# One merged scan per pair of states, a fourth ring group, and another order of feed-forward units around the output projection

## The reference

```python
# part 1: selective state space model, inner width 1024, 16 states
xz = x @ W_in + b_in;  u, z = split(xz);  u = silu(u)
B, C = split(u @ W_xproj + b_xproj);  dt = softplus(u @ W_dt + b_dt)
h[t] = h[t-1] * exp(dt[t] * A) + dt[t] * u[t] * B[t]      # per channel and state
y[t] = sum over states of h[t] * C[t] + D * u[t]
x = layernorm(x + (y * silu(z)) @ W_out + b_out)
# part 2: masked cross attention, 16 heads, context of 77
# part 3: x @ W1 + b1, plus gain * sin(theta + 0.1 * hidden), relu, @ W2 + b2
```

## Time and profile before

| | us |
|---|---|
| median of 3 timed runs (3167.78 to 3171.23) | 3168.35 |
| the profiled execution, device time | 3163.83 |
| its span, first to last instruction | 3162.1 |
| scan phase, first scan to last (from the trace) | 59.0 to 1964.2 |

### The profile page before, as it was taken

The page is one execution under the profiler, slowest core; times in us unless marked ns, Lnnn a source line. Parts: engine busy times, 40 slices in busy tenths (PEclk is TensorE's granted clock), DMA queues, the critical chain, the costliest instruction groups (busy, mean ns, idle before and its releaser), DMA issues. The chain is left out here.

```text
span 3162.1 us, 48953 instructions
## 1 busy us (share of the span) xinstructions
PE 2830.4 (90%) x18968; PEld 1268.4 (40%) x18968; DVE 2692.5 (85%) x3070; ACT 2015.1 (64%) x3616; POOL 1828.9 (58%) x944
## 2 busy tenths in 40 slices
PE   7878878978878888888889889989999999999998
PEld 2222222222222222222222223556666676667765
DVE  5899999999999999999999978766666677777776
ACT  6766776776776776776776745555555556655564
POOL 4788988978978988978988987311111111112100
PEclk9999999999999999999999989999999999999999
DMA  4111112112112111111112143701111000000000
GB/s 159 51 51 41 58 51 66 45 37 71 41 43 65 41 51 57 50 41 57 51 53 65 51 131 125 225 28 42 42 42 42 28 29 22 23 30 29 30 8 14
DMA packets 119976, 172.51 MB, mean 55 GB/s; under 512 B 13250, under 2 KB 48706, under 8 KB 119236
## 3 DMA queue, kind: packets, MB, share of 16 engines
q1 hardware_dynamic: 119748, 169.37, 16.5%
HBM read 100.66 MB, written 66.58 MB: 53 GB/s over the span
## 5 line engine op out<-in xcount | busy, mean ns | idle before, releaser
L852 POOL TENSOR_TENSOR h<-h,c_rep 128x1024 f32<-128x1024 f32 x511 | 1196.7, 2355 | 281.6 <-ACT carry L605 280.1
L756 DVE TENSOR_TENSOR_SCAN h<-r_ps,carry,h 128x512 f32<-128x512 f32 x768 | 938.9, 1262 | 10.6 <-ACT r_ps L599 10.4
L599 ACT ACTIVATE r_ps<-r_ps,decay 128x512 f32<-128x512 f32 x1024 | 631.7, 656 | 390.3 <-PE r_ps L361 389.8
L743 DVE TENSOR_TENSOR h<-u_ps,b_rep 128x1024 f32<-128x1024 f32 x512 | 614.0, 1199 | 48.0 <-PE u_ps L374 47.4
L374 PE MATMUL u_ps<-dtu,spread 32*128 32x512 f16 x2048 | 319.5, 390 | 105.3 <-DVE h L743 105.0
L361 PE MATMUL r_ps<-dt,spread 32*128 32x512 f16 x2048 | 316.9, 387 | 49.7 <-DVE h L756 43.1
L390 PE MATMUL y_ps<-h,gather 128*32 128x512 f32 x2048 | 288.4, 637 | 65.8 <-POOL h L852 64.7
L1882 POOL TENSOR_TENSOR o_in<-o_in,rows 128x1024 f32<-128x1024 f32 x15 | 37.0, 2464 | 508.9 <-DMA o_in<-o_dram 508.9
L756 DVE TENSOR_TENSOR_SCAN h<-r_ps,zero,h 128x512 f32<-128x512 f32 x256 | 313.1, 1263 | 7.1 <-ACT r_ps L599 7.0
L40 PE MATMUL fps<-x,region 128*128 128x256 f16 x1024 | 283.6, 277 | 3.4 <-issue 2.4
L41 PE MATMUL fps<-x,region 128*128 128x256 f16 x1024 | 283.0, 276 | 0.0
(11 more groups left out here) (260 smaller groups left out, 5635.0 us busy)
## 6 DMA issues: line engine op xcount, KB each, us to landing
u_t_dram<-u SPq DMA_DIRECT2D x16, 1024.0 KB, 4.7
uz<-u_t_dram SPq DMA_DIRECT2D x64, 256.0 KB, 4.0
z_t_dram<-zs SPq DMA_DIRECT2D x32, 512.0 KB, 3.0
uz<-z_t_dram SPq DMA_DIRECT2D x64, 256.0 KB, 4.1
y_t_dram<-y SPq DMA_DIRECT2D x64, 256.0 KB, 2.3
region<-y_t_dram SPq DMA_DIRECT2D x32, 256.0 KB, 3.3
result<-x SPq DMA_DIRECT2D x16, 512.0 KB, 2.8
x_t<-dram_x_t SPq DMA_DIRECT2D x15, 512.0 KB, 4.0
```

Source lines behind the costliest of these rows:

```text
L599: nc.scalar.activation(bank, bank, ACT.Exp, scale=decay[:, col:col + 1]).then_inc(s_da, 1)
L743: nc.vector.tensor_tensor(h[:, g % H_GROUPS, o:o + 2, :], u_ps[:, :, :], b_rep[:, c % 2:c % 2 + 1, :].broadcast_to([P, 2, TS]), ALU.mult). ...
L756: nc.vector.tensor_tensor_scan(row, r_ps[:, 2 * (pair % 2) + o, :], row, start, ALU.mult, ALU.add)\
L852: nc.gpsimd.tensor_tensor(rows, rows, c_rep[:, c % 2:c % 2 + 1, :].broadcast_to([P, 2, TS]), ALU.mult)\
```

## The change

In the scan phase, `scans` becomes one instruction of 1024 columns over both banks. Between the two rows the state must be cut and restarted. So PE writes zero into column 0 of the second bank's decays by a one-column matmul (`joint_decay_zero`), after the exponentials. In chunks that carry a state over, ACT first adds decay times carry into column 0 of the second row (`joint_column`). PE does this step after `produce` and before `sums` and `rep_dt`. The ring gets a fourth group, `sums` and `gate` come two pairs later, `y` is written over the z tile in `uz`, and `rep_dt` and `save_carry` count scans by the pair. In the second phase, bodies with `ops` move feed-forward steps of units 0 to 4 around the projection and the scores on PE, ACT and DVE, and `body(1)`'s loads and bias for chunk 2 are issued in `first()`.

```diff
-H_GROUPS = 3
+H_GROUPS = 4
+SUMS_BEHIND = 5
@@ SP: load_z
-                    sp.wait_ge(s_y, n - 1)
+                    sp.wait_ge(s_yout[n % 2], 16 * (n // 2))
@@ PE
                 if pair >= 2:
-                    pe.wait_ge(s_scan, 2 * pair - 2)
+                    pe.wait_ge(s_scan, pair - 1)
...
+            def joint_decay_zero(pair):
+                c, j, p = place(pair)
+                pe.wait_ge(s_da, 2 * pair + 2)
+                if c % PER_SEQ:
+                    pe.wait_ge(s_joint, joints(pair) + 1)
+                nc.tensor.matmul(r_ps[:, 2 * (pair % 2) + 1, 0:1], spread[0:32, 0, :], no_decay, start=True, stop=True)\
+                    .then_inc(s_cut, 1)
...
                     out_piece((s - OUT_AT) // 2, (s - OUT_AT) % 2)
-                if pair % 2 and pair >= 3:
-                    sums((pair - 3) // 2)
+                if pair + 1 < TOTAL:
+                    joint_decay_zero(pair + 1)
+                if pair % 2 and pair >= SUMS_BEHIND:
+                    sums((pair - SUMS_BEHIND) // 2)
                 if pair + 2 < TOTAL:
                     rep_dt(pair + 2)
+            sums(TOTAL // 2 - 2)
             sums(TOTAL // 2 - 1)
@@ ACT
+            def joint_column(pair):
+                c, j, p = place(pair)
+                if c % PER_SEQ == 0:
+                    return
+                act.wait_ge(s_da, 2 * pair + 2)
+                act.wait_ge(s_m1, pair + 1)
+                act.wait_ge(s_carry, pair - PAIRS + 1)
+                col = j * NSTATE + 2 * p + 1
+                at = h[:, pair // 2 % H_GROUPS, 2 * (pair % 2) + 1, 0:1]
+                nc.scalar.activation(at, r_ps[:, 2 * (pair % 2) + 1, 0:1], ACT.Identity, bias=at,
+                                     scale=carry[:, col:col + 1]).then_inc(s_joint, 1)
...
                     exps(pair + 2)
+                    joint_column(pair + 2)
@@ DVE
-                for o in range(2):
-                    col = j * NSTATE + 2 * p + o
-                    dve.wait_ge(s_da, 2 * pair + o + 1)
-                    row = h[:, pair // 2 % H_GROUPS, 2 * (pair % 2) + o, :]
-                    start = carry[:, col:col + 1] if c % PER_SEQ else zero[:, 0:1]
-                    nc.vector.tensor_tensor_scan(row, r_ps[:, 2 * (pair % 2) + o, :], row, start, ALU.mult, ALU.add)\
-                        .then_inc(s_scan, 1)
+                dve.wait_ge(s_cut, pair + 1)
+                o = 2 * (pair % 2)
+                col = j * NSTATE + 2 * p
+                rows = h[:, pair // 2 % H_GROUPS, o:o + 2, :].rearrange("p o t -> p (o t)")
+                start = carry[:, col:col + 1] if c % PER_SEQ else zero[:, 0:1]
+                nc.vector.tensor_tensor_scan(rows, r_ps[:, o:o + 2, :].rearrange("p o t -> p (o t)"), rows, start,
+                                             ALU.mult, ALU.add).then_inc(s_scan, 1)
...
-                if pair % 8 == 2 and pair >= 10:
+                if pair % 8 == 4 and pair >= 12:
                     gate(pair // 8 - 1)
@@ second phase, SP: first()
+                sp.wait_ge(s_x1, 1)
+                load(o_in[:, :, :], chunk_rows("o", 2), s_oin)
...
+                sp.wait_ge(s_rwo, NT)
+                load(x1[:, 0, :, :], chunk_rows("x", 2), s_xin)
@@ PE: body with ops
                         out_projection(c, m * NT + 1, sps)
+                    hidden(b, 2)
                     scores(c, 0, batch, (0, 1), ops)
+                    hidden(b, 3)
+                    scores(c, 0, batch, (2, 3), ops)
+                    second(b, 0)
+                    scores(c, 1, batch, (0, 1), ops)
+                    hidden(b, 4)
+                    scores(c, 1, batch, (2, 3), ops)
+                    second(b, 1)
@@ ACT: body, not late
-                    y_high(Y_PAIRED - 1)
                     weights_high(8)
                     weights_high(9)
+                    y_high(Y_PAIRED - 1)
@@ ACT: body with ops
+                    if not late:
+                        deviation("x1", 0, c + 2)
+                    sine(b, 0)
                     out_evacuated(m * NT, sps)
+                    sine(b, 1)
+                    relu(b, 0)
+                    relu(b, 1)
                     out_evacuated(m * NT + 1, sps)
+                    hid_out(b, 2)
+                    sine(b, 2)
+                    hid_out(b, 3)
+                    sine(b, 3)
+                    relu(b, 2)
+                    relu(b, 3)
+                    exps(c, 0)
+                    exps(c, 1)
+                    hid_out(b, 4)
@@ DVE: body with ops
+                    fraction(b, 0)
+                    fraction(b, 1)
+                    if not late:
+                        statistics("x1", 0, c + 1, x1[:, 1 - par, :, :])
+                        normalize("x1", 0, c + 1, x1[:, 1 - par, :, :])
+                    mix(b, 0)
+                    mix(b, 1)
+                    act_low(b, 0)
+                    act_low(b, 1)
                     masked(c, 0, (0, 1))
+                    fraction(b, 2)
                     masked(c, 0, (2, 3))
+                    row_maximum(c, 0)
+                    mix(b, 2)
+                    fraction(b, 3)
                     masked(c, 1, (0, 1))
+                    less_maximum(c, 0)
@@ POOL: first() and body
-                for i in range(1, Y_PAIRED - 1):
+                for i in range(1, Y_PAIRED - 2):
                     y_low(i)
+                o_bias(2)
+                y_low(Y_PAIRED - 2)
...
-                if more:
+                if more and late:
                     pool.wait_ge(s_avl, c * NT)
                     o_bias(c + 1)
...
+                if not late:
+                    for m in ops:
+                        y_low(m * NT + 1)
                 x2_bias(c - 1, 1 - par)
-                for m in ops:
-                    y_low(m * NT + 1)
```

More of the change, by code:

```diff
@@ L1356, in body @@
                     hidden(b, 1)
-                if front:
-                    scores(c, 0, batch, (2, 3), ops)
-                hidden(b, 2)
-                if front:
-                    scores(c, 1, batch, (0, 1), ops)
-                hidden(b, 3)
-                if front:
-                    scores(c, 1, batch, (2, 3), ops)
-                second(b, 0)
-                hidden(b, 4)
-                second(b, 1)
+                    if front:
+                        scores(c, 0, batch, (2, 3), ())
+                    hidden(b, 2)
+                    if front:
+                        scores(c, 1, batch, (0, 1), ())
+                    hidden(b, 3)
+                    if front:
+                        scores(c, 1, batch, (2, 3), ())
+                    second(b, 0)
+                    hidden(b, 4)
+                    second(b, 1)
                 hidden(b, 5)
@@ L1813, in body @@
                     normalize("w2", 2, d, x2[:, par, :, :])
[L1814 to L1816 removed]
+                    if more:
+                        normalize("x1", 0, c + 1, x1[:, 1 - par, :, :])
+                if ops:
+                    fraction(b, 0)
+                    fraction(b, 1)
+                    if not late:
+                        statistics("x1", 0, c + 1, x1[:, 1 - par, :, :])
+                        normalize("x1", 0, c + 1, x1[:, 1 - par, :, :])
+                    mix(b, 0)
+                    mix(b, 1)
+                    act_low(b, 0)
+                    act_low(b, 1)
@@ L1839, in body @@
                     less_maximum(c, 1)
-                mix(b, 3)
-                fraction(b, 4)
-                act_low(b, 3)
+                    fraction(b, 4)
+                else:
+                    if front:
+                        masked(c, 0, (0, 1))
+                    fraction(b, 0)
+                    if front:
+                        masked(c, 0, (2, 3))
+                    fraction(b, 1)
+                    mix(b, 0)
+                    if front:
+                        masked(c, 1, (0, 1))
+                        row_maximum(c, 0)
+                    fraction(b, 2)
+                    act_low(b, 0)
+                    mix(b, 1)
+                    if front:
+                        masked(c, 1, (2, 3))
+                        less_maximum(c, 0)
+                    act_low(b, 1)
+                    fraction(b, 3)
+                    mix(b, 2)
+                    if front:
+                        row_maximum(c, 1)
+                    act_low(b, 2)
+                    if front:
+                        less_maximum(c, 1)
+                    mix(b, 3)
+                    fraction(b, 4)
+                    act_low(b, 3)
@@ L1922, in body @@
                     x1_sum(c + 1, 1 - par)
+                if not late:
+                    for m in ops:
+                        y_low(m * NT + 1)
                 x2_bias(c - 1, 1 - par)
-                for m in ops:
-                    y_low(m * NT + 1)
+                if late:
+                    for m in ops:
+                        y_low(m * NT + 1)
             all_chunks(pool, first, body)
```

67 lines of the change are left out of this document (27 added, 40 removed).

## The result

| | before | after |
|---|---|---|
| median of 4 timed runs, us | 3168.07 (3164.61 to 3171.23) | 3217.91 (3213.28 to 3221.38) |
| profiled execution, us | 3163.83 | 3213.28 |
| scan phase, first scan to last | 1905.2 | 1981.9 |

The ratio is 1.0157, 95% interval 1.0139 to 1.0174: the change makes the kernel 1.6% slower. 3132 was forecast, with a range up to 3185. The phases moved in opposite directions: the scan phase took 76.7 us more, the second phase (from the last scan to the end) 25.6 us less.

What follows compares the result with a forecast made beforehand. DVE was taken to set the scan phase's pace and PE to bound its last pairs and the second phase. -56 - 30 + 67 + 5 - 14 - 8 = -36 us gave 3132 us, range 3070 to 3185.

Steps and rivals of the forecast that it cites:

- The merged scan: DVE, scan phase: one instruction start saved per pair, 0.116 us x 482 pairs = -56 us, bounds -17 and -90.
- Chain length: Scan phase, from the second exponential's end to the scan: 0.6 us, or 0.35 in chunks 0 and 4 without joint column.
- Most pairs have the decays one to three us early, so it is covered there: Scan phase: the new chain of 0.6 us is covered in most pairs, but not behind a SiLU.
- only a late ACT makes it wait: PE at the cut: it arrives 1.8 to 2.4 us after `rep_dt`, while exponentials and column need 1.5.
- The price of a SiLU: Scan phase: the new chain costs 1.2 us behind each of 56 SiLUs, +67 us, bounds +17 and +140.
- The walk through one burst: Scan phase from pair 35, worked through behind a SiLU: pair 38 is 1.1 us late, pair 39 0.6, the next burst 1.5.
- The fourth group, the later sums: Scan phase: sums two pairs later end PE's waits for POOL and DVE's for `u_ps`, -30 us, bounds -20 and -45.
- 30 of the 47.4: Scan phase: of DVE's 47.4 us of waits for `u_ps` from PE, 30 us were taken as saved.
- Moving `gate` and writing y over z cost nothing: Scan phase: `load_z` now waits for the store of y, but has over 27 us until its gate; no cost.
- PE at the end of the phase: Last 30 pairs of the scan phase, bound by PE: the cut costs 30 x 0.17 = +5 us.
- The second phase: Bodies with `ops`: holes before the scores and slow clock go, -14 us in bodies 2 to 6, -8 in body 1, together -22.
- The rival: Scan phase: the cut makes PE and ACT one queue at the slower side's pace; 2.5 us a SiLU, 3205 us, 13%.

Runs made afterwards that it cites:

- cut_two_scans: `sp_order` with the merged scan split into two of 512 columns that follow without a wait, cut and joint column kept: 3215.26 us, 1.0153.
- no_silu: `sp_order` with a plain copy in place of each SiLU and no table loads around it: 3100.96 us, 0.9791.
- two_scans_sp: After with two scans again, no cut or joint column, and in the last chunk the store of y behind the output tiles: 3124.58 us, 0.9877.
- sp_order: After with only SP's store of y in the last chunk moved behind the output tiles' traffic: 3202.58 us, 1.0117.
- act_zero: `sp_order` with the zero written by ACT behind its joint column instead of by PE's cut: 3194.73 us, 1.0091.
- ffn_only: The scan phase of before with the second phase of after: 3141.11 us, 0.9929.
- col_no_wait: `two_scans_sp`, first scan waiting for both exponentials, plus an ACT instruction of the joint column's shape on unused data that no scan waits for: 3159.42 us, 0.9978.

## Why the prediction was wrong

The failed steps are in the scan phase. The prediction held the new chain covered in most pairs and cheap behind a SiLU (1.2 us), and so counted the merged scan's saving in full. The runs showed a chain that is short of cover in far more pairs, about 2 us a SiLU, 11 of the forecast 56 us from merging, and 24 us in the last chunk from a queue that it hadn't looked at.

- **The merged scan** was sized well: its record is 2.342 us (2.33 forecast), an undisturbed pair 3.375 (3.36), so 0.106 us a pair are saved. Forecast were -56 us. The step that failed is "0.116 x 482 pairs": it assumed that DVE sets the pace afterwards too. `cut_two_scans` shows that 11 us arrive. The 157 ns that the prediction took from the Trainium skill ("VectorE: DVE Perf Modes", section on the TRN2 errata) did not show either: 106 ns are the measured return.
- **Chain length.** The sum said 0.6 us, the trace has 0.82, the median of the 106 pairs in which each step followed the one before at once. The 201 ns of `save_carry` were the wrong row for the joint column: it takes 351. The hand-over behind it took 0.145 and the one from the cut to the scan 0.137, not 0.05. The exponential that they were read from ends at 679.80 in the trace, 0.13 before its scan and not under 0.1. Without the joint column the forecast 0.35 stands beside 0.34. For the cut itself 0.17 was right (0.163 to 0.166).
- **"Most pairs have the decays one to three us early, so it is covered there"** and "only a late ACT makes it wait" put the chain at nothing outside the bursts. In chunks 2 to 6 of after PE stood behind the joint column 153 times, in the 256 pairs that have one. Without any SiLU 7.9 us of excess a chunk are left (`no_silu`), where `two_scans_sp`, without the chain but with its SiLUs, has 2.9.
- **The price of a SiLU**, 1.2 us x 56 = +67, is the term that was mis-sized. Two numbers bear on it: 2.0 us a SiLU by `no_silu`, and chunks 1 to 3, 5 and 6 with an excess that grew by 16.7, 2.1 a SiLU, although ring and sums took some off. Neither is quite the term: the first holds what a SiLU had cost before as well (0.3 by the prediction's reading of the earlier trace rows, so 1.7 would be left), the second also what does not come from SiLUs. The walk through one burst gave 1.1 and 0.6 for the two pairs behind it, because it let PE go on at full speed and with `sums` at 1.07. In the trace PE stood for 3.3 us, was granted 0.50, and the two pairs lost 1.93 and 2.05. That the clock is what turns one stall into two is read from one burst of the trace; no experiment held the clock fixed. Over chunks 1 to 6 the clock was at half for 112.6 us before and 146.8 after, but from kernel to kernel this time does not go with the loss: it is 174.1 in `sp_order` and 221.9 in `act_zero`, whose chunks are no longer.
- **The loop that I hadn't closed.** The prediction walked the new chain forwards only. It is part of a loop over two pairs, since `r_ps` holds two: scan(k), `rep_dt(k+2)`, `exps(k+2)`, scan(k+2). Before, it needed 2.37 for the scans, 1.03 for four spread matmuls (three of 0.215 and one of 0.388), 0.61 for the first exponential and some 0.2 of hand-overs, 4.2 of 2 x 3.48 = 7.0 us. After, it needs 2.34 + 1.03 + 1.23 + 0.82 + 0.2 = 5.6 of 2 x 3.375 = 6.75. The slack fell from 2.7 to 1.1 us. Into it must go what stands ahead in the queues: `sums` with 1.07 on PE, an emptying of `pj` or the skip product with 0.7 on ACT, six matmuls of `produce`. This is worked out, not tested by itself, but it agrees with the steps: 9 us for 0.6 longer, 23 and 13 for the next 0.35 on ACT and the wait for it, 42 for the last 0.4 (from 709.01 to 709.45 in the burst), which also holds up PE's queue, and 11 of 54 for a shorter pair.
- **The fourth group, the later sums:** -30 forecast, -16.5 measured (`two_scans_sp` against `ffn_only`). The step "such waits are gone" holds: PE has none for POOL left. But "30 of the 47.4" of DVE's waits was too much: 14.8 of 23.5 us in chunks 2 to 6 are still there without them, behind other causes.
- **"Moving `gate` and writing y over z cost nothing"** failed. I asked who waits for y's buffer, and not what is queued behind SP's wait for `gate`. In the last chunk that queue also feeds the projection: 24 us, shown by `sp_order`.
- **PE at the end of the phase:** +5 forecast for the cut. The last 30 pairs took 130.9 us before and 134.6 in `sp_order`, but 136.6 in `two_scans_sp`, which has no cut. So they did get longer, and the cut is not what did it; the cause stays open.
- **The second phase:** -22 forecast, -22.5 measured by `ffn_only`. Bodies 2 to 6 gave -20 instead of -14, body 1 -2.4 there (-5.2 in after) instead of -8, so the fit of the total is in part luck. The 2.8 us a body came from the bodies without `ops`, which had 0.9 us of PE's idle time themselves (258.42 busy of 262.00); after has none. In body 1 the late second `out_evacuated` cost its 2.6 us as expected, and the 3.2 for DVE's `x` had not been seen.
- **The rival** of one queue for PE and ACT named the right place and gave 3205 at 2.5 us a SiLU, from 1.85 on slower. The measured price, 1.7 to 2.1, lies about that point, and I had given it 13%. With SP's 24 us and what the chain costs outside the bursts the kernel came out slower. The mechanism was half right: in the burst shown the next pair's work does stand behind PE's cut, but `act_zero` shows that freeing PE does not cure it.

In sum, the scan phase was forecast at -14 and came at +77. Of these 91 us, 24 are SP's order. Some 54 are chunks 1 to 3, 5 and 6, where the unfulfilled part of the merged scan's saving shows as excess and is not to be added again: their excess was forecast at about 12.4 (6.5 before, 9.6 for the SiLUs, less 3.7 for ring and sums) and is 23.2, 5 x 10.8 more. Of the other 13, 5 are the merged scan's 0.106 in place of 0.116 us over 482 pairs; the rest is spread over chunks 0, 4 and 7 and stays without a cause of its own.

## What to carry to other kernels

Before an instruction is saved on the engine that sets the pace, close the loop through the buffers it needs and write down its slack; here 0.6 us more cost 9 us over the kernel at the start, and 0.4 us more, in PE's queue, cost 42 once little slack was left. Behind a moved step, look at every in-order queue that waits for it, the DMA queue's too, and ask what stands behind. Where one part of a change is dear and the others pay, try the others alone: here they were 1.3% faster than before.

## What the runs showed of the hardware

- Time on ACT does not go by the number of elements alone. A 128x1 activation with scale and bias as columns and its input in PSUM takes 351 ns, the same with its input in SBUF 389 (`col_no_wait`), a 128x2 Copy 201 ns.

```profile
L628 ACT ACTIVATE h<-r_ps,h,carry 128x1 f32<-128x1 f32 x64 | 22.5, 351 | 2.1
```

- A matmul of one column has a record of 163 to 166 ns. From the end of the joint column to its start there are 0.145 us, from the end of an exponential (chunk 4) 0.055. The Trainium skill ("VectorE: DVE Perf Modes", clock table) gives a matmul max(60, 6+N) cycles, 25 ns for one column. No record here is that short; for 512 columns the same formula gives 216 ns, which agrees with the 0.215 from start to start and not with the record of 0.38, so it is a pace and not the length of a record.
- A scan of 1024 columns takes 2342 ns, two of 512 take 1262 each, but from start to start merging returns only 106 ns.
- A hole of 3.3 us on PE was followed by 3.45 us at a granted clock of 0.50, in the middle of a phase in which PE is busy nine tenths of the time.
